# Epsilon of z moved into the bias of the Square, and GpSimd's scaling of t written as one product

## The chip, the cores and the metric

The kernel runs on one core of one Trainium2 chip. The metric is the device time of one execution in microseconds; of the kernel before three runs are known, 151.21, 151.26 and 151.44, with a median of 151.26. The profile is of one further execution, whose instructions span 149.9 us from the first to the last.

Five engines work side by side, each with its own queue of instructions that it takes strictly in order: TensorE (PE in the profile), VectorE (DVE), ScalarE (ACT), GpSimd (POOL) and SyncE (SP, which only issues DMAs here). Between engines there are only semaphores: an instruction adds to one when it is done, and another engine waits until it has reached a count.

## The reference

The input x has 32 sequences of 256 tokens with 128 channels. Two blocks follow each other, both of the form x + layernorm(block(layernorm(x))):

```python
# block 1
A_t = sigmoid(A_param)[:, None] ** t[None, :]
K   = C_vec * A_t * B_vec                       # a causal filter of 256 taps for each channel
out = conv(x_t, K)[..., :L] + D_vec * x_t
out = gelu(out) @ W_proj.T + b_proj
y   = layer_norm(x + out, gamma, beta)          # (z - mean) * rsqrt(var + 1e-5) * gamma + beta
# block 2
xr = mu_r * x + (1 - mu_r) * x_prev             # x_prev: the token before
xk = mu_k * x + (1 - mu_k) * x_prev
out = sigmoid(xr @ W_r.T) * (square(relu(xk @ W_k.T)) @ W_v.T)
```

With the four plain layer norms around the blocks and the one inside block 1 there are five normalisations, and each needs a variance, an epsilon and the power of -0.5 for every token.

## The kernel before

The 8192 tokens are cut into 16 units of 512 (two sequences, four tiles of 128 tokens on the partitions). Everything is fp32 and x stays in SBUF. For one unit u the work is this chain, with the names of the code:

- DVE takes the statistics of x; POOL makes x_r = (var + eps) ** -0.5 and x_bias (`x_scale_of`, for two units at a time); ACT normalises (`normalise`) into xn.
- POOL multiplies xn by powers of A (`xn_times_pow`, 128x512), PE forms prefix sums of it (`prefix_sum`) and transposes xn (`transpose_xn`); DVE turns both into the convolution (`convolve`); ACT applies gelu; PE projects and adds (`project`), which gives z, already with mean zero over the channels, in PSUM (ps_z0 to ps_z2 in turn).
- ACT squares z with a scale of 128 ** -0.5 and adds up along the channels (`square_z`, L397), which gives the variance z_var. POOL adds epsilon (`z_variance`, L248, writing z_ve) and takes the power of -0.5 (`z_root`, L253, writing z_r). DVE uses z_r (`scale_z`), takes the statistics of y, POOL makes yf_r of them, DVE adds y to x (`residual`, giving t) and takes t's statistics.
- POOL makes t_r (`t_variance`, `t_root`). Then t is scaled by t_r into t_scaled: for units 1, 3, 5, 7, 9, 10, 11 and 13 by POOL (`scale_t_pool`, L324), for the others by ACT (`scale_t`, L405). PE transposes it (`transpose_t`, L854), ACT copies it out (`copy_tT`), and PE forms keys, gates and values (L863, L874, L884).
- DVE gates the values, takes statistics of f; POOL makes the last root and out_bias; ACT scales f, POOL subtracts it from x (`add_f`) and SP stores. Units 11, 12, 13 and 15 take a way over DVE at the end.

The order on each engine is written out by hand as one list of calls per engine (L331 to L356 for POOL, L480 on for ACT, L745 on for DVE, L889 on for PE), so that the units run as a staggered pipeline. An engine that meets an unfulfilled wait holds up everything behind it in its list. Buffers come in rings of D = 4 units.

Of the kernel before, what the change touches and what calls it, by code (L numbers as in the profile page):

```python
# [14 lines left out]
def sandwich(nc, x, A_param, B_vec, C_vec, D_vec, W_proj, b_proj, gamma, beta, W_r, W_k, W_v, mu_r, mu_k, out):  # L15
    fp32 = mybir.dt.float32
    ALU = mybir.AluOpType
# [3 lines left out]
    D = 4  # L21
# [9 lines left out]
    with ctx:  # L31
        def sb(name, *shape):
            return ctx.enter_context(nc.sbuf_tensor(name, [P, *shape], fp32))
# [12 lines left out]
        centre = sb("centre", P)  # L46
        prefix_ones = sb("prefix_ones", SEQ)
        neg_half = sb("neg_half", 2 * TILES)
        eps_tile = sb("eps_tile", 2 * TILES)
        zero_col = sb("zero_col", 1)  # L50
        act_warm = sb("act_warm", 2)
        a_col, b_col, c_col, d_col, proj_col, bias_col = (sb(n, 1) for n in (
# [23 lines left out]
        tsT = ring("tsT", 2, SEQ + 1)  # L76
        k_act, tanh, f, f_normal = ring("k_act", UW), ring("tanh", UW), ring("f", UW), ring("f_normal", UW)
        junk = ring("junk", UW)
        z_var, z_ve, z_r = (sb(n, UNITS * TILES) for n in ("z_var", "z_ve", "z_r"))
        t_raw = sb("t_raw", UNITS * TILES, 3)  # L80
        yf_raw = sb("yf_raw", UNITS, 2, TILES, 3)
        yf_r, yf_mean_r = sb("yf_r", UNITS, 2, TILES), sb("yf_mean_r", UNITS, 2, TILES)
# [23 lines left out]
            "xn_ready", "xn_pow_ready", "xT_ready", "xT_copied"))  # L106
        prefix_ready, scaled_ready, conv_ready, gelu_ready = (sem(n) for n in (
            "prefix_ready", "scaled_ready", "conv_ready", "gelu_ready"))
        z_ready, z_squares, z_ve_done, z_scale, z_gamma, y_ready = (sem(n) for n in (
            "z_ready", "z_squares", "z_ve_done", "z_scale", "z_gamma", "y_ready"))  # L110
        y_stats, y_ve_done, y_scale, t_ready = (sem(n) for n in ("y_stats", "y_ve_done", "y_scale", "t_ready"))
        t_stats, t_ve_done, t_scale, ts_ready, ts_pool_ready, tT_ready, tT_copied = (sem(n) for n in (
            "t_stats", "t_ve_done", "t_scale", "ts_ready", "ts_pool_ready", "tT_ready", "tT_copied"))
# [84 lines left out]
        def _(pool):  # L198
# [1 line left out]
            g_.memset(ident[:], 0.0).then_inc(s_filled, 1)  # L200
            g_.memset(prefix_ones[:], 1.0).then_inc(s_filled, 1)
            g_.memset(neg_half[:], -0.5)
            g_.memset(eps_tile[:], EPS)
            for r in range(D):
                g_.memset(tsT[r][:, :, 0:1], 0.0)
            pool.wait_ge(s_filled, 2)
# [26 lines left out]
            def xn_times_pow(u):  # L233
                if u == 0:
                    pool.wait_ge(s_pow, 1)
                pool.wait_ge(xn_ready, u + 1)
                after(pool, prefix_ready, u - D + 1)
                g_.tensor_tensor(xn_pow[u % D][:].rearrange("p (q l) -> p q l", l=SEQ),  # L238
                                 xn[u % D][:].rearrange("p (q l) -> p q l", l=SEQ),
                                 pow_token[:, None, :].to_broadcast([P, 2, SEQ]), ALU.mult).then_inc(xn_pow_ready, 1)  # L240
# [2 lines left out]

                return neg_half[:, 0:n * TILES].rearrange("p (n j) -> p n j", j=TILES)

            def z_variance(u, n):
                pool.wait_ge(z_squares, u + n)
                g_.tensor_tensor(cols(z_ve, u, n), cols(z_var, u, n), eps_tile[:, 0:n * TILES],  # L248
                                 ALU.add).then_inc(z_ve_done, n)

            def z_root(u, n):
                pool.wait_ge(z_ve_done, u + n)
                g_.tensor_tensor(cols(z_r, u, n), cols(z_ve, u, n), neg_half[:, 0:n * TILES],  # L253
                                 ALU.pow).then_inc(z_scale, n)

            def y_variance(u, n):
# [63 lines left out]
            def scale_t_pool(u):  # L320
                pool.wait_ge(t_scale, u + 1)
                after(pool, tT_ready, u - D + 1)
                for j in range(TILES):
                    last = g_.tensor_scalar(tile(t_scaled[u % D], j), xa(u, j), col(t_r, u, j), 1.0, ALU.mult, ALU.mult)  # L324
                last.then_inc(ts_pool_ready, 1)

            def add_f(u):
                pool.wait_ge(f_scaled, u + 1 if u < FUSED[0] else u)
# [2 lines left out]
            x_scale_tiles(0, 0, 2)  # L331
            x_scale_tiles(1, 2, 4)
            x_scale_of(1, 1, 1); xn_times_pow(0); x_scale_of(2, 2, 2); xn_times_pow(1); x_scale_of(3, 4, 2)
            xn_times_pow(2); xn_times_pow(3); z_variance(0, 1); z_root(0, 1); x_scale_of(4, 6, 2); z_variance(1, 1)
            z_root(1, 1); y_variance(0, 1); y_root(0, 1); xn_times_pow(4); x_scale_of(5, 8, 2); y_variance(1, 1)
            t_variance(0, 1); y_root(1, 1); xn_times_pow(5); z_variance(2, 2); t_root(0, 1); z_root(2, 2)
            xn_times_pow(6); t_variance(1, 1); t_root(1, 1); xn_times_pow(7); y_variance(2, 2); y_root(2, 2)
            scale_t_pool(1); xn_times_pow(8); x_scale_of(6, 10, 2); t_variance(2, 2); z_variance(4, 2); t_root(2, 2)
            z_root(4, 2); f_variance(0, 1); f_root(0, 1); scale_t_pool(3); yf_means(0, 1); xn_times_pow(9)
            y_variance(4, 2); out_biases(0, 1); y_root(4, 2); xn_times_pow(10); add_f(0); x_scale_of(7, 12, 2)  # L340
            t_variance(4, 2); z_variance(6, 2); t_root(4, 2); z_root(6, 2); f_variance(1, 1); xn_times_pow(11)
            scale_t_pool(5); f_root(1, 1); yf_means(1, 1); y_variance(6, 2); out_biases(1, 1); y_root(6, 2)
# [16 lines left out]
        def _(act):  # L359
# [568 lines left out]
```

## Time and profile before

| what | value |
|---|---|
| three runs, us | 151.21, 151.26, 151.44 (median 151.26) |
| span of the profiled execution, us | 149.9 |
| PE busy, us | 135.8 (91%) |
| DVE busy, us | 131.5 (88%) |
| ACT busy, us | 129.7 (87%) |
| POOL busy, us | 132.5 (88%) |
| mean granted TensorE clock | 0.984 |

The median of the runs lies 1.36 us above the span of the profiled execution. All four compute engines are busy for nearly nine tenths of the span, so the shares alone do not say which of them sets the end. The chain that ended last and the idle time of an engine before a single instruction, with what ended it, say more. In a row of the timeline stand the start in us, the length in us (of several instructions together where "xN" is above 1), engine, line, operation, output<-inputs, and in brackets the idle time before and what released the engine. The lengths of neighbouring rows can overlap by up to about 0.1 us.

### The profile page before, as it was taken

The numbers are of one execution on the slowest core, as the hardware profiler recorded it, in microseconds if no ns is written. First come the engines' busy times: TensorE is split into PE (matmuls) and PEld (weight loads), VectorE is DVE, ScalarE is ACT, GpSimd is POOL, SyncE is SP. The second block draws the span as 40 slices with busy tenths as digits, with TensorE's granted clock in tenths as the row PEclk, the third lists the DMA queues.
The fourth block names the chain that finished last, engine by engine and source line by source line (L and its number), as shares of the span: only waits on it lengthen the run. The fifth ranks groups of instructions, "written<-read, shape, count | busy, mean of one in ns | idle before, by whom it ended". The sixth has DMA issues, their size and how long they took to land.

```text
span 149.9 us, 3292 instructions
## 1 busy us (share of the span) xinstructions
PE 135.8 (91%) x950; PEld 116.2 (78%) x950; DVE 131.5 (88%) x372; ACT 129.7 (87%) x388; POOL 132.5 (88%) x211
## 2 busy tenths in 40 slices
PE   6777888979999999999999999999999999999900
PEld 6666877867797889797989797988887887777900
DVE  0969899989999998999998999998999899339981
ACT  4869999799879999979779999959998988999940
POOL 4589999999899999999999999888999999999282
PEclk9999999999999999999999999999999999999985
DMA  3999930000000002000200001300200100406524
GB/s 78 239 289 240 294 94 0 0 2 4 0 0 0 0 4 72 0 2 0 74 0 0 0 4 47 98 0 0 77 0 0 56 14 0 142 5 194 157 73 140
DMA packets 18705, 8.99 MB, mean 60 GB/s; under 512 B 1536, under 2 KB 18688, under 8 KB 18688
## 3 DMA queue, kind: packets, MB, share of 16 engines
q1 hardware_dynamic: 17840, 8.52, 20.3%
q10 hardware_dynamic: 848, 0.26, 0.8%
q8 instruction: 8, 0.13, 0.4%
q14 instruction: 9, 0.07, 0.1%
HBM read 4.59 MB, written 4.19 MB: 59 GB/s over the span
## 4 chain that ended last, share of the span: by engine, by line
PE 70%; POOL 17%; DMA 3%; issue 2%; DVE 2%; SPq 2%; POOLq 1%
PE ps_k L863 9%; PE ps_k L864 9%; PE ps_r L875 9%; PE ps_r L874 9%; PE ps_tv L884 9%; PE ps_z L841 7%; POOL xn_pow L238 5%; PE ps_tv L854 4%; POOL x_r L229 4%; PE ps_prefix L821 4%; DMA x_all<-in_x 3%; PE ps_z L842 3%; PE ps_xT L813 3%; POOL z_r L253 2%; PE ps_prefix L827 2%
## 5 line engine op out<-in xcount | busy, mean ns | idle before, releaser
L377 ACT ACTIVATE xn<-x_all,x_bias,x_r 128x128 f32<-128x128 f32 x64 | 26.4, 494 | 0.6 <-POOL x_bias L220 0.6
L875 PE MATMUL ps_r<-mixed_T,tsT 128*128 128x128 f32 x128 | 24.7, 275 | 0.0
L874 PE MATMUL ps_r<-mixed_T,tsT 128*128 128x128 f32 x128 | 24.7, 275 | 0.0
L841 PE MATMUL ps_z<-pv_T,gelu 128*128 128x128 f32 x128 | 22.1, 275 | 0.0
L434 ACT ACTIVATE f_normal<-f,out_bias,yf_r 128x128 f32<-128x128 f32 x48 | 19.7, 492 | 1.6 <-POOL out_bias L292 1.6
L238 POOL TENSOR_TENSOR xn_pow<-xn,pow_token 128x512 f32<-128x512 f32 x16 | 20.3, 1272 | 0.0
L874 PEld LDWEIGHTS ps_r<-mixed_T,tsT 128*128 128x128 f32 x128 | 19.5, 192 | 0.5 <-issue 0.5
L841 PEld LDWEIGHTS ps_z<-pv_T,gelu 128*128 128x128 f32 x128 | 19.4, 191 | 0.5 <-issue 0.5
L397 ACT ACTIVATE junk<-ps_z 128x128 f32<-128x128 f32 x64 | 16.7, 277 | 3.2 <-PE ps_z L842 3.2
L875 PEld LDWEIGHTS ps_r<-mixed_T,tsT 128*128 128x128 f32 x128 | 19.4, 192 | 0.0
L580 DVE SCALAR_TENSOR_TENSOR ps_z<-ps_z,z_r,beta_row 128x128 f32<-128x128 f32 x64 | 17.5, 353 | 0.5 <-POOL z_r L253 0.5
L592 DVE SCALAR_TENSOR_TENSOR x_all<-ps_z,yf_r,x_all 128x128 f32<-128x128 f32 x64 | 17.4, 344 | 0.2 <-POOL yf_r L263 0.2
L842 PE MATMUL ps_z<-ident,xnT 128*128 128x128 f32 x64 | 17.4, 273 | 0.0
L884 PEld LDWEIGHTS ps_tv<-pv_T,k_act 128*128 128x128 f32 x124 | 15.4, 192 | 1.9 <-issue 1.9
L821 PE MATMUL ps_prefix<-prefix_ones,xn_pow 128*128 128x256 f32 x48 | 14.8, 389 | 2.0 <-POOL xn_pow L238 1.9
L863 PE MATMUL ps_k<-tsT,mixed_T 128*128 128x512 f32 x32 | 16.5, 599 | 0.0
L884 PE MATMUL ps_tv<-pv_T,k_act 128*128 128x128 f32 x124 | 16.4, 275 | 0.0
L864 PE MATMUL ps_k<-tsT,mixed_T 128*128 128x512 f32 x32 | 16.3, 592 | 0.0
L329 POOL TENSOR_TENSOR x_all<-x_all,f_normal 128x512 f32<-128x512 f32 x12 | 15.2, 1277 | 0.3 <-ACT f_normal L434 0.3
L263 POOL TENSOR_TENSOR yf_r<-y_ve,neg_half 128x8 f32<-128x8 f32 (+1 forms) x10 | 13.9, 1390 | 0.6 <-issue 0.2
L253 POOL TENSOR_TENSOR z_r<-z_ve,neg_half 128x8 f32<-128x8 f32 (+1 forms) x10 | 13.8, 1385 | 0.6
L272 POOL TENSOR_TENSOR t_r<-t_ve,neg_half 128x8 f32<-128x8 f32 (+1 forms) x10 | 13.9, 1387 | 0.2
(114 smaller groups left out, 365.7 us busy)
## 6 DMA issues: line engine op xcount, KB each, us to landing
out_x<-x_all SPq DMA_DIRECT2D x15, 256.0 KB, 2.3
x_all<-in_x SPq DMA_DIRECT2D x7, 512.0 KB, 6.3
x_all<-in_x SPq DMA_DIRECT2D x2, 128.0 KB, 2.9
x_all<-in_x SPq DMA_DIRECT2D x1, 256.0 KB, 3.3
out_x<-x_all SPq DMA_DIRECT2D x1, 128.0 KB, 1.8
out_x<-x_all ACTq DMA_DIRECT2D x1, 128.0 KB, 1.9
w_pv<-in_W_proj ACTq DMA_DIRECT2D x1, 64.0 KB, 3.5
w_pv<-in_W_v ACTq DMA_DIRECT2D x1, 64.0 KB, 4.3
```

The source lines that it names most:

```text
L238: g_.tensor_tensor(xn_pow[u % D][:].rearrange("p (q l) -> p q l", l=SEQ), xn[u % D][:].rearrange("p (q l) -> p q l", l=SEQ), pow_token[:, ...
L377: last = a_.activation(tile(xn[u % D], j), xa(u, j), ACT.Identity, bias=col(x_bias, u, j), scale=col(x_r, u, j))
L434: last = a_.activation(tile(f_normal[u % D], j), tile(f[u % D], j), ACT.Identity, bias=out_bias[:, u, j:j + 1], scale=yf_r[:, u, 1, j:j + 1])
L580: last = v_.scalar_tensor_tensor(tile(ps_z[u % 3], j), tile(ps_z[u % 3], j), col(z_r, u, j), beta_row[:], ALU.mult, ALU.add)
L821: t_.matmul(ps_prefix[:, q * SEQ:(q + 1) * SEQ], tile(xn_pow[u % D], 2 * q), prefix_ones[:], start=True, stop=False)
L841: t_.matmul(tile(ps_z[u % 3], j), tile(gelu[u % D], j), pv_T[:, 0, :], start=True, stop=False)
L842: last = t_.matmul(tile(ps_z[u % 3], j), tile(xnT[u % D], j), ident[:], is_transpose=True, start=False, stop=True)
L863: t_.matmul(k_out, mixed_T[:, 2, :], tsT[u % D][:, :, 1:SEQ + 1], start=True, stop=False)
L864: t_.matmul(k_out, mixed_T[:, 3, :], tsT[u % D][:, :, 0:SEQ], start=False, stop=True).then_inc(k_ready, 1)
L874: t_.matmul(tile(ps_r, j), tsT[u % D][:, q, l + 1:l + 1 + P], mixed_T[:, 0, :], start=True, stop=False)
L875: last = t_.matmul(tile(ps_r, j), tsT[u % D][:, q, l:l + P], mixed_T[:, 1, :], start=False, stop=True)
L884: last = t_.matmul(tile(bank, j), tile(k_act[u % D], j), pv_T[:, 1, :], start=True, stop=True)
```

## The change

Two things are rewritten; what is computed stays the same up to rounding.

First, epsilon of z. The sum over the channels of (z / sqrt(128) + b) ** 2 is the variance plus 2 b / sqrt(128) times the sum of z plus 128 b ** 2. The sum of z is zero, and with b = sqrt(eps / 128) the last term is eps. So the Square gets this number as its bias, its accumulated output is the variance with epsilon in it, and the ten calls of `z_variance` go with their tile z_ve, their constant tile eps_tile and their semaphore. `z_root` now waits for the Squares itself. The Squares no longer wait for z_ve.

Second, `scale_t_pool`: four scalings of 128x128 by a column of t_r become one product of 128x512 with the four columns of t_r broadcast along the channels.

```diff
@@ POOL
-            g_.memset(eps_tile[:], EPS)
...
-            def z_variance(u, n):
+            def z_root(u, n):
                 pool.wait_ge(z_squares, u + n)
-                g_.tensor_tensor(cols(z_ve, u, n), cols(z_var, u, n), eps_tile[:, 0:n * TILES],
-                                 ALU.add).then_inc(z_ve_done, n)
-
-            def z_root(u, n):
-                pool.wait_ge(z_ve_done, u + n)
-                g_.tensor_tensor(cols(z_r, u, n), cols(z_ve, u, n), neg_half[:, 0:n * TILES],
+                g_.tensor_tensor(cols(z_r, u, n), cols(z_var, u, n), neg_half[:, 0:n * TILES],
                                  ALU.pow).then_inc(z_scale, n)
...
             def scale_t_pool(u):
                 pool.wait_ge(t_scale, u + 1)
                 after(pool, tT_ready, u - D + 1)
-                for j in range(TILES):
-                    last = g_.tensor_scalar(tile(t_scaled[u % D], j), xa(u, j), col(t_r, u, j), 1.0, ALU.mult, ALU.mult)
-                last.then_inc(ts_pool_ready, 1)
+                g_.tensor_tensor(t_scaled[u % D][:].rearrange("p (j c) -> p j c", c=P),
+                                 xa(u, 0, TILES).rearrange("p (j c) -> p j c", c=P),
+                                 cols(t_r, u)[:, :, None].to_broadcast([P, TILES, P]), ALU.mult).then_inc(ts_pool_ready, 1)
...
-            t_variance(0, 1); y_root(1, 1); xn_times_pow(5); z_variance(2, 2); t_root(0, 1); z_root(2, 2)
+            t_variance(0, 1); y_root(1, 1); xn_times_pow(5); t_root(0, 1); z_root(2, 2)
...
@@ ACT
             def square_z(u):
                 act.wait_ge(z_ready, u + 1)
-                after(act, z_ve_done, u - D + 1)
...
-                    last = a_.activation(tile(junk[u % D], j), tile(ps_z[u % 3], j), ACT.Square, scale=float(P) ** -0.5,
-                                         accum_out=col(z_var, u, j))
+                    last = a_.activation(tile(junk[u % D], j), tile(ps_z[u % 3], j), ACT.Square, bias=(EPS / P) ** 0.5,
+                                         scale=float(P) ** -0.5, accum_out=col(z_var, u, j))
```

The calls of `z_variance` are struck from POOL's list and nothing else in it changes place. How POOL's instructions then stand is seen at two places, and ACT's at one. The first place is on POOL, from the powers of units 2 and 3 to the root of y of unit 0 (z_r with four columns is one unit's root). Before:

```order
L238 TENSOR_TENSOR xn_pow<-xn,pow_token 128x512 x2
L248 TENSOR_TENSOR z_ve<-z_var,eps_tile 128x4
L253 TENSOR_TENSOR z_r<-z_ve,neg_half 128x4
L226 TENSOR_SCALAR x_v<-x_raw 128x8
L227 TENSOR_SCALAR x_neg<-x_raw 128x8
L229 TENSOR_TENSOR x_r<-x_v,neg_half 128x8
L231 TENSOR_TENSOR x_bias<-x_neg,x_r 128x8
L248 TENSOR_TENSOR z_ve<-z_var,eps_tile 128x4
L253 TENSOR_TENSOR z_r<-z_ve,neg_half 128x4
L258 TENSOR_SCALAR y_ve<-yf_raw 128x4
```

The same place on POOL after the change:

```order
L236 TENSOR_TENSOR xn_pow<-xn,pow_token 128x512 x2
L246 TENSOR_TENSOR z_r<-z_var,neg_half 128x4
L224 TENSOR_SCALAR x_v<-x_raw 128x8
L225 TENSOR_SCALAR x_neg<-x_raw 128x8
L227 TENSOR_TENSOR x_r<-x_v,neg_half 128x8
L229 TENSOR_TENSOR x_bias<-x_neg,x_r 128x8
L246 TENSOR_TENSOR z_r<-z_var,neg_half 128x4
L251 TENSOR_SCALAR y_ve<-yf_raw 128x4
```

Two additions of epsilon are gone, and the roots of z read the Squares' sums directly. The second place is on POOL, from the powers of unit 5 to the scaling of t of unit 1 (z_r with eight columns is of units 2 and 3). Before:

```order
L238 TENSOR_TENSOR xn_pow<-xn,pow_token 128x512
L248 TENSOR_TENSOR z_ve<-z_var,eps_tile 128x8
L272 TENSOR_TENSOR t_r<-t_ve,neg_half 128x4
L253 TENSOR_TENSOR z_r<-z_ve,neg_half 128x8
L238 TENSOR_TENSOR xn_pow<-xn,pow_token 128x512
L267 TENSOR_SCALAR t_ve<-t_raw 128x4
L272 TENSOR_TENSOR t_r<-t_ve,neg_half 128x4
L238 TENSOR_TENSOR xn_pow<-xn,pow_token 128x512
L258 TENSOR_SCALAR y_ve<-yf_raw 128x8
L263 TENSOR_TENSOR yf_r<-y_ve,neg_half 128x2x4
L324 TENSOR_SCALAR t_scaled<-x_all,t_r 128x128 x4
```

The same place on POOL after the change:

```order
L236 TENSOR_TENSOR xn_pow<-xn,pow_token 128x512
L265 TENSOR_TENSOR t_r<-t_ve,neg_half 128x4
L246 TENSOR_TENSOR z_r<-z_var,neg_half 128x8
L236 TENSOR_TENSOR xn_pow<-xn,pow_token 128x512
L260 TENSOR_SCALAR t_ve<-t_raw 128x4
L265 TENSOR_TENSOR t_r<-t_ve,neg_half 128x4
L236 TENSOR_TENSOR xn_pow<-xn,pow_token 128x512
L251 TENSOR_SCALAR y_ve<-yf_raw 128x8
L256 TENSOR_TENSOR yf_r<-y_ve,neg_half 128x2x4
L316 TENSOR_TENSOR t_scaled<-x_all,t_r 128x512
```

The addition of epsilon and its wait for the Squares of unit 3 no longer stand ahead of t_r of unit 0, and t_scaled is one instruction with two tensors as its inputs. The third place is on ACT, around the Squares of unit 0 after the change; a bias or a scale that is a tile stands among an instruction's inputs:

```order
L370 ACTIVATE xn<-x_all,x_bias,x_r 128x128 x4
L384 ACTIVATE gelu<-conv 128x512
L379 ACTIVATE xnT<-ps_xT,bias_col 128x512
L370 ACTIVATE xn<-x_all,x_bias,x_r 128x128 x4
L389 ACTIVATE junk,z_var<-ps_z 128x128 x4
```

Nothing moved there: the Squares read ps_z alone, as before, and their new bias is a number in the instruction, not a tile.

## Rows read from the trace of the kernel before

**Rows 1.** Page, chain of work that ended last: shares of the span by engine.

```profile
PE 70%; POOL 17%; DMA 3%; issue 2%; DVE 2%; SPq 2%; POOLq 1%
```

**Rows 2.** Busy time by stretch: stretch and length, then busy us (instructions) per engine.

```profile
10.30:35.45 25.15, 21.22 (x156) 18.81 (x154) 23.70 (x60) 22.99 (x79) 23.87 (x35) 1.00 0.40 105
35.45:140.05 104.60, 104.60 (x733) 88.21 (x734) 95.97 (x269) 95.84 (x288) 98.00 (x146) 1.00 0.10 30
140.05:149.90 9.85, 2.74 (x25) 2.55 (x23) 6.07 (x18) 4.13 (x10) 4.55 (x9) 0.76 0.40 121
```

**Rows 3.** Timeline of PE, 31 to 43 us: start, length, engine, line, operation.

```profile
31.47 0.70 PE L821 MATMUL ps_prefix<-prefix_ones,xn_pow 128*128 128x256 f32 x2 [0.99 <-POOL xn_pow L238]
...
34.21 0.60 PE L854 MATMUL ps_tv<-ident,t_scaled 128*128 128x128 f32 x4
34.71 0.63 PE L813 MATMUL ps_xT<-ident,xn 128*128 128x128 f32 x4
35.45 0.70 PE L821 MATMUL ps_prefix<-prefix_ones,xn_pow 128*128 128x256 f32 x2
...
42.11 0.60 PE L854 MATMUL ps_tv<-ident,t_scaled 128*128 128x128 f32 x4
```

**Rows 4.** Timeline of POOL, 18 to 42 us.

```profile
18.85 0.20 POOL L248 TENSOR_TENSOR z_ve<-z_var,eps_tile 128x4 f32<-128x4 f32 x1
19.13 1.01 POOL L253 TENSOR_TENSOR z_r<-z_ve,neg_half 128x4 f32<-128x4 f32 x1
...
22.55 0.20 POOL L248 TENSOR_TENSOR z_ve<-z_var,eps_tile 128x4 f32<-128x4 f32 x1
22.82 1.01 POOL L253 TENSOR_TENSOR z_r<-z_ve,neg_half 128x4 f32<-128x4 f32 x1
...
31.38 0.20 POOL L248 TENSOR_TENSOR z_ve<-z_var,eps_tile 128x8 f32<-128x8 f32 x1
31.54 1.00 POOL L272 TENSOR_TENSOR t_r<-t_ve,neg_half 128x4 f32<-128x4 f32 x1
...
34.12 1.28 POOL L238 TENSOR_TENSOR xn_pow<-xn,pow_token 128x512 f32<-128x512 f32 x1
...
40.21 1.43 POOL L324 TENSOR_SCALAR t_scaled<-x_all,t_r 128x128 f32<-128x128 f32 x4
```

**Rows 5.** Timeline of ACT, 32 and 77 us: two waits.

```profile
32.58 1.28 ACT L405 ACTIVATE t_scaled<-x_all,t_r 128x128 f32<-128x128 f32 x4 [0.29 <-POOL t_r L272]
...
77.49 0.69 ACT L386 ACTIVATE xnT<-ps_xT,bias_col 128x512 f32<-128x512 f32 x1 [0.84 <-PE ps_xT L813]
```

**Rows 6.** Timeline of DVE at 33 us, the first half of convolution 5.

```profile
33.09 0.69 DVE L550 TENSOR_TENSOR conv_scaled<-ps_prefix,pow_down 128x512 f32<-128x512 f32 x1 [0.47 <-PE ps_prefix L823]
```

**Rows 7.** Waits of POOL: who waited for whom, us in total, times, longest.

```profile
POOL x_r L218 <- DVE x_v L526: 2.2, 1, 2.2
```

**Rows 8.** Timeline of DVE, 133 to 141 us.

```profile
133.75 0.70 DVE L619 SCALAR_TENSOR_TENSOR ps_z<-tanh,ps_tv 128x512 f32<-128x512 f32 x1 [3.35 <-ACT tanh L427]
...
137.22 0.69 DVE L634 TENSOR_TENSOR ps_z<-ps_z,yf_raw 128x512 f32<-128x512 f32 x1
137.92 0.69 DVE L610 TENSOR_TENSOR x_all<-x_all,ps_xT 128x512 f32<-128x512 f32 x1
138.75 1.13 DVE L654 SCALAR_TENSOR_TENSOR x_all<-ps_z,yf_r,x_all 128x128 f32<-128x128 f32 x4
...
140.58 0.68 DVE L605 SCALAR_TENSOR_TENSOR f<-tanh,ps_tv 128x512 f32<-128x512 f32 x1
```

**Rows 9.** Timeline of POOL at 137 us, the root of f of units 12 and 13.

```profile
136.98 1.63 POOL L282 TENSOR_TENSOR yf_r<-f_ve,neg_half 128x8 f32<-128x8 f32 x1
```

**Rows 10.** Groups of ACT's instructions: line, operation, xcount, busy us, mean ns.

```profile
L397 ACT ACTIVATE junk<-ps_z 128x128 f32<-128x128 f32 x64 | 16.7, 277 | 3.2 <-PE ps_z L842 3.2
...
L386 ACT ACTIVATE xnT<-ps_xT,bias_col 128x512 f32<-128x512 f32 x16 | 11.0, 685 | 3.5 <-PE ps_xT L813 3.5
...
L412 ACT ACTIVATE tsT<-ps_tv 128x512 f32<-128x512 f32 x16 | 9.4, 590 | 1.8 <-PE ps_tv L854 1.8
```

More of the change, by code:

```diff
@@ L48, in sandwich @@
         neg_half = sb("neg_half", 2 * TILES)
-        eps_tile = sb("eps_tile", 2 * TILES)
         zero_col = sb("zero_col", 1)
@@ L78, in sandwich @@
         junk = ring("junk", UW)
-        z_var, z_ve, z_r = (sb(n, UNITS * TILES) for n in ("z_var", "z_ve", "z_r"))
+        z_var, z_r = (sb(n, UNITS * TILES) for n in ("z_var", "z_r"))
         t_raw = sb("t_raw", UNITS * TILES, 3)
@@ L108, in sandwich @@
             "prefix_ready", "scaled_ready", "conv_ready", "gelu_ready"))
-        z_ready, z_squares, z_ve_done, z_scale, z_gamma, y_ready = (sem(n) for n in (
-            "z_ready", "z_squares", "z_ve_done", "z_scale", "z_gamma", "y_ready"))
+        z_ready, z_squares, z_scale, z_gamma, y_ready = (sem(n) for n in (
+            "z_ready", "z_squares", "z_scale", "z_gamma", "y_ready"))
         y_stats, y_ve_done, y_scale, t_ready = (sem(n) for n in ("y_stats", "y_ve_done", "y_scale", "t_ready"))
@@ L333, in _ @@
             x_scale_of(1, 1, 1); xn_times_pow(0); x_scale_of(2, 2, 2); xn_times_pow(1); x_scale_of(3, 4, 2)
-            xn_times_pow(2); xn_times_pow(3); z_variance(0, 1); z_root(0, 1); x_scale_of(4, 6, 2); z_variance(1, 1)
+            xn_times_pow(2); xn_times_pow(3); z_root(0, 1); x_scale_of(4, 6, 2)
             z_root(1, 1); y_variance(0, 1); y_root(0, 1); xn_times_pow(4); x_scale_of(5, 8, 2); y_variance(1, 1)
-            t_variance(0, 1); y_root(1, 1); xn_times_pow(5); z_variance(2, 2); t_root(0, 1); z_root(2, 2)
+            t_variance(0, 1); y_root(1, 1); xn_times_pow(5); t_root(0, 1); z_root(2, 2)
@@ L337, in _ @@
             xn_times_pow(6); t_variance(1, 1); t_root(1, 1); xn_times_pow(7); y_variance(2, 2); y_root(2, 2)
-            scale_t_pool(1); xn_times_pow(8); x_scale_of(6, 10, 2); t_variance(2, 2); z_variance(4, 2); t_root(2, 2)
+            scale_t_pool(1); xn_times_pow(8); x_scale_of(6, 10, 2); t_variance(2, 2); t_root(2, 2)
             z_root(4, 2); f_variance(0, 1); f_root(0, 1); scale_t_pool(3); yf_means(0, 1); xn_times_pow(9)
             y_variance(4, 2); out_biases(0, 1); y_root(4, 2); xn_times_pow(10); add_f(0); x_scale_of(7, 12, 2)
-            t_variance(4, 2); z_variance(6, 2); t_root(4, 2); z_root(6, 2); f_variance(1, 1); xn_times_pow(11)
+            t_variance(4, 2); t_root(4, 2); z_root(6, 2); f_variance(1, 1); xn_times_pow(11)
@@ L342, in _ @@
             scale_t_pool(5); f_root(1, 1); yf_means(1, 1); y_variance(6, 2); out_biases(1, 1); y_root(6, 2)
-            xn_times_pow(12); add_f(1); x_scale_of(8, 14, 2); z_variance(8, 2); z_root(8, 2); f_variance(2, 2)
+            xn_times_pow(12); add_f(1); x_scale_of(8, 14, 2); z_root(8, 2); f_variance(2, 2)
             t_variance(6, 2); xn_times_pow(13); t_root(6, 2); scale_t_pool(7); y_variance(8, 2); y_root(8, 2)
             xn_times_pow(14); f_root(2, 2); xn_times_pow(15); yf_means(2, 2); t_variance(8, 2); out_biases(2, 2)
-            z_variance(10, 2); z_root(10, 2); add_f(2); t_root(8, 2); add_f(3); y_variance(10, 2); f_variance(4, 2)
+            z_root(10, 2); add_f(2); t_root(8, 2); add_f(3); y_variance(10, 2); f_variance(4, 2)
@@ L347, in _ @@
             y_root(10, 2); scale_t_pool(9); f_root(4, 2); yf_means(4, 2); out_biases(4, 2); t_variance(10, 2)
-            z_variance(12, 2); z_root(12, 2); add_f(4); t_root(10, 2); scale_t_pool(10); y_variance(12, 2)
-            f_variance(6, 2); y_root(12, 2); f_root(6, 2); z_variance(14, 1); yf_means(6, 2); z_root(14, 1)
-            out_biases(6, 2); scale_t_pool(11); t_variance(12, 2); z_variance(15, 1); t_root(12, 2); add_f(5)
+            z_root(12, 2); add_f(4); t_root(10, 2); scale_t_pool(10); y_variance(12, 2)
@@ L351, in _ @@
+            f_variance(6, 2); y_root(12, 2); f_root(6, 2); yf_means(6, 2); z_root(14, 1)
+            out_biases(6, 2); scale_t_pool(11); t_variance(12, 2); t_root(12, 2); add_f(5)
             z_root(15, 1); y_variance(14, 1); f_variance(8, 2); y_root(14, 1); f_root(8, 2); yf_means(8, 2)
```

## Prediction

> **What bounds the kernel now.** I read the chain that ended last first: TensorE holds 70% of it and GpSimd 17% [rows 1]. The reader is to ask where these two parts lie, since only GpSimd is to lose work. The busy time by stretch answers it [rows 2]. From 35.45 us to 140.05 us PE is busy for 104.60 of 104.60 us: whatever the others save there, PE has no idle time to give up, and this stretch can only move as a block. Before it, from 10.30 to 35.45, PE is busy for 21.22 of 25.15 us and POOL for 23.87. PE's own timeline names what it waits for there: 0.99 us for POOL's xn_pow ahead of the prefix sum of unit 5 at 31.47, and at 35.45, where the dense stretch begins, the prefix sum of unit 6 starts 0.05 us after xn_pow of unit 6 ends at 34.12 + 1.28 = 35.40 [rows 3, 4]. So POOL's queue sets when PE's block begins, PE sets when it ends, and after 140.05 a chain over DVE, POOL and ACT closes the kernel.
>
> **The change part by part.** Removed are ten additions of epsilon, three of them ahead of 35.45. What one is worth there is the step from its start to that of the next instruction in POOL's queue, since nothing else was awaited:
> - unit 0: 18.85 to 19.13, 0.28 us; unit 1: 22.55 to 22.82, 0.27 us. The root that follows needs the sum, so the handing over within POOL goes too.
> - units 2 and 3: 31.38 to 31.54, 0.16 us; here t_r of unit 0 stood between, and no handing over was seen [rows 4].
>
> Together 0.71 us, of which 0.55 fall ahead of xn_pow of unit 5 and all 0.71 ahead of xn_pow of unit 6, which then ends at 34.69.
>
> Does PE take it? The prefix sum of unit 5 goes from 31.47 to 30.92, since PE had been idle for 0.99 us. The project of unit 4 and the transposes of t of unit 0 follow on PE, the latter at 34.21 - 0.55 = 33.66. They need t_scaled from ACT. ACT began it at 32.58 after 0.29 us of waiting for t_r [rows 5]; t_r now comes 0.55 + 0.16 us earlier, so ACT begins at 32.29 and ends 1.28 us later at 33.57, just in time. The transposes of xn of unit 6 started at 34.71. They also need convolution 5 by DVE. Its first half waited 0.47 us for the prefix sum of unit 5 [rows 6], so DVE can move by that 0.47 and no more; the transposes start at 34.24 and, with the 0.44 us that the four of t take before them (34.21 to 34.65), leave PE free at 34.68. xn_pow of unit 6 is handed over at 34.74. So POOL is still last, by 0.06 us, and PE's block begins 0.71 us earlier. A handful of hundredths decide here, so the lower end of this term is the 0.47 of DVE.
>
> The seven other additions of epsilon, 0.20 us each, lie beside PE's full block and give nothing by themselves. The same holds for the removed memset of eps_tile at the start: POOL waits 2.2 us for DVE right after its setup [rows 7]. The twelve waits that ACT loses were for sums long done; I take nothing for them, and a gain would be hidden behind PE as well.
>
> Added is the bias of the Square. No row shows a Square with one. From below, ACT's copies show what an operand can cost: 685 ns for 512 elements with bias_col as the bias, 590 ns without it, so 95 ns for each; the Square now takes 277 ns [rows 10]. The bound is 0 to 95 ns. The new bias is a number that the instruction carries, where the old one carried a zero, and its inputs are the same single tile, so I take 0. The Trainium skill has the same distinction (ScalarE: Activation LUTs, What ACT_TABLE_LOAD costs): immediate scale and bias are the base price and each column operand adds about 93 ns; the 95 ns of this trace agrees, and by that rule this bias adds nothing.
>
> Moved is the scaling of t on POOL, eight times: four scalings took 1.43 us in all, a product of two 128x512 tensors (xn_pow, one of them broadcast over the sequences) takes 1.28 [rows 4]. What no row of POOL shows is an input that stands still along the innermost dimension. On DVE such a product costs nothing extra: 0.69 us for centring by a broadcast column at 137.22, 0.69 us for the plain subtraction behind it [rows 8]. I take 1.28; the range for it is 1.28 to 2.56, the latter if both halves of the traffic doubled. The first product has the least room: t_scaled of unit 1 began at 40.21, and I let it come only DVE's 0.47 earlier, at 39.74. PE wants it at 42.11 - 0.71 = 41.40 [rows 3]. So it may take 1.6 us before PE feels it, and eight times 0.15 us saved beside PE's block are worth nothing.
>
> The Trainium skill has a rule that could speak against this (GPSIMD Engine Reference, Performance pitfalls for Q7 kernels): an inner step of more than 8 bytes makes a read about half as dear again. A step of zero is not named there. No run here shows it on POOL; as an estimate by that page's factor the product would take 1.28 x 1.5 = 1.92 us, 0.3 us beyond what unit 1 has room for.
>
> At the end, what moves with PE is ACT's tanh of unit 13, for which DVE waits 3.35 us at 133.75; the DVE chain after it sets the end. In it add_fused (138.75) begins 0.14 us after DVE's instruction before is over (137.92 + 0.69 = 138.61), and POOL's root of f ends at 138.61 too [rows 8, 9]. POOL is further ahead by then, so I count these 0.14 us as gained: gate(14) at 140.58 follows on DVE, and the statistics, roots and store follow on it.
>
> **Sum.** 0.71 + 0.14 = 0.85 us off the profiled span of 149.9, which becomes about 149.05. The median of the runs lies 1.36 us above that span, before the first and after the last instruction, where nothing changes: 151.26 - 0.85 = 150.4.
>
> **Rivals.**
> - DVE cannot follow. Only 0.47 us of the advance survives because the convolutions feed PE through the block's first units and DVE is busy there nearly as much as PE (95.97 of 104.60 us) [rows 2]. 151.26 - 0.47 = 150.8. Against it: DVE has 8.6 us of idle time in the block.
> - The gain is given back inside the block: ACT (95.84 of 104.60 us) does not move, and PE waits for it until it is where it was. 151.26, no change. Against it: ACT itself waits for PE within the block, 0.84 us at 77.49 [rows 5], so it follows PE rather than leads.
> - The product with a broadcast column is dear on POOL. At 1.92 us (the factor of the skill's rule) unit 1's transposes lose 0.3 us, 8 x 0.49 - 7 x 0.2 = 2.5 us more POOL work vanish in its 6.6 us of idle time, and 0.55 us of 0.85 remain: 150.7. At 2.56 us unit 1 ends at 42.30, 0.9 us too late, and the 0.71 are more than lost; 8 x 1.13 - 1.4 = 7.6 us of additional work exceed the 6.6 us of idle time by 1.0: 151.26 + 0.2 to + 1.0, some 152, and up to 157 if the idle time cannot be used because it sits in waits. It turns slower above 39.74 + 2.3 us. For it speaks only that no row of POOL shows the pattern; against it the DVE row.
> - The Square's bias is fetched like a column after all: 64 x 95 ns = 6.1 us on ACT, which has 8.8 us idle in the block. Between nothing lost and 4 us lost, some 153. Against it: the instruction has no second tile.
>
> **How the numbers follow.** Forecast (150.1 to 150.6): 0.58. DVE follows by half, or a product of about 1.9 us (150.6 to 150.9): 0.18. Given back (151.0 to 151.5): 0.14. Dear product: 0.07. Dear bias: 0.03. What a measurement of this kernel can tell from no change is about 0.2%, 0.3 us. So faster 0.76, same 0.14, slower 0.10. The range leaves out the two slower cases and what of the forecast's spread lies beneath it: 150.1 to 151.2; the likeliest case's own is 150.1 to 150.6.
>
> **What would show it.** Right: POOL's z_r of unit 0 begins near 18.85, xn_pow of unit 6 near 33.4, PE's prefix sum of unit 6 near 34.74, PE's waits in the block stay absent, and its dense stretch is 104.6 us long; Squares of 277 ns; t_scaled in one instruction of about 1.28 us. Wrong: Squares nearer 370 ns, t_scaled above 1.6 us with PE idle before the transposes at L854, or a PE block that begins earlier and ends where it did. If the block begins 0.7 us earlier and the end does not, the step that failed is that ACT and DVE follow PE.

## The result, and the profile after

The changed kernel takes 150.28 us (median of 4 runs, 150.21 to 150.56) against 151.24 us before on the same chip (151.13 to 151.44): a ratio of 0.9932, 95% interval 0.9915 to 0.9949, so 0.96 us less by the medians (0.77 to 1.29 by the interval). The forecast was 150.4. The profiled execution took 150.25 us, its span 148.5 us (149.9 before; why the spans differ by more than the times is told further down).

The busy time by stretch, cut where PE's dense stretch begins and as many microseconds behind (columns as in [rows 2]):

```profile
10.30:34.20 23.90, 20.94 (x154) 18.66 (x153) 23.06 (x59) 22.42 (x78) 22.93 (x31) 1.00 0.35 104
34.20:138.80 104.60, 104.60 (x734) 88.20 (x734) 95.38 (x270) 96.14 (x289) 93.62 (x115) 1.00 0.10 30
138.80:148.50 9.70, 2.75 (x25) 2.56 (x23) 6.05 (x17) 4.14 (x10) 4.55 (x9) 0.81 0.41 121
```

PE's dense stretch is as long as before, 104.60 us without idle time; it begins at 34.20 and not at 35.45, 1.25 us earlier. POOL does 4.4 us less in it, 93.62 for 98.00, and the stretch is no shorter for it. The time came from ahead of the stretch. POOL's timeline there (start, length, operation):

```profile
10.28 1.65 POOL L227 TENSOR_TENSOR x_r<-x_v,neg_half 128x8 f32<-128x8 f32 x1
...
18.31 1.01 POOL L246 TENSOR_TENSOR z_r<-z_var,neg_half 128x4 f32<-128x4 f32 x1
...
21.73 1.01 POOL L246 TENSOR_TENSOR z_r<-z_var,neg_half 128x4 f32<-128x4 f32 x1
...
31.27 1.64 POOL L246 TENSOR_TENSOR z_r<-z_var,neg_half 128x8 f32<-128x8 f32 x1
32.87 1.28 POOL L236 TENSOR_TENSOR xn_pow<-xn,pow_token 128x512 f32<-128x512 f32 x1
...
38.99 1.04 POOL L316 TENSOR_TENSOR t_scaled<-x_all,t_r 128x512 f32<-128x512 f32 x1
```

and the same x_r in the kernel before:

```profile
10.82 1.65 POOL L229 TENSOR_TENSOR x_r<-x_v,neg_half 128x8 f32<-128x8 f32 x1
```

From x_r of units 2 and 3 to xn_pow of unit 6, POOL needed 34.12 - 10.82 = 23.30 us before [rows 4] and needs 32.87 - 10.28 = 22.59 now: 0.71 less. Another 0.54 us lie ahead of that x_r: POOL begins the whole queue earlier. PE, DVE and ACT at the places of [rows 3, 5, 6]:

```profile
30.39 0.70 PE L813 MATMUL ps_prefix<-prefix_ones,xn_pow 128*128 128x256 f32 x2 [0.46 <-POOL xn_pow L236]
...
33.63 0.63 PE L805 MATMUL ps_xT<-ident,xn 128*128 128x128 f32 x4
34.20 0.70 PE L813 MATMUL ps_prefix<-prefix_ones,xn_pow 128*128 128x256 f32 x2
```

```profile
31.59 1.30 ACT L397 ACTIVATE t_scaled<-x_all,t_r 128x128 f32<-128x128 f32 x4
```

```profile
32.01 0.69 DVE L542 TENSOR_TENSOR conv_scaled<-ps_prefix,pow_down 128x512 f32<-128x512 f32 x1
```

PE's wait for xn_pow of unit 5 fell from 0.99 to 0.46 us, and the waits of ACT (0.29) and DVE (0.47) are gone. The prefix sum of unit 6 again starts 0.05 us after its xn_pow ends (32.87 + 1.28 = 34.15), so POOL still sets the start of the stretch.

What came earlier ahead of x_r is seen on POOL's x_v, which needs DVE's statistics, and on DVE, which waits for the loads of x. POOL before (the same x_v is at 9.84 after, without a wait, right behind xn_pow, which ends at 9.76):

```profile
10.37 0.20 POOL L226 TENSOR_SCALAR x_v<-x_raw 128x8 f32<-128x8 f32 x1 [0.49 <-DVE x_raw L514]
```

DVE's statistics of units 2 to 5, before:

```profile
8.85 1.43 DVE L514 BATCH_NORM_STATS2 x_raw<-x_all 128x6 f32<-128x256 f32 x4 [0.85 <-DMA x_all<-in_x]
10.62 1.43 DVE L514 BATCH_NORM_STATS2 x_raw<-x_all 128x6 f32<-128x256 f32 x4 [0.34 <-DMA x_all<-in_x]
```

and after, with a shorter wait for the first load and none for the second:

```profile
8.26 2.95 DVE L506 BATCH_NORM_STATS2 x_raw<-x_all 128x6 f32<-128x256 f32 x8 [0.38 <-DMA x_all<-in_x]
```

At the end of the kernel (DVE, then POOL):

```profile
136.69 0.69 DVE L602 TENSOR_TENSOR x_all<-x_all,ps_xT 128x512 f32<-128x512 f32 x1 [0.27 <-ACT ps_xT L438]
137.47 1.13 DVE L646 SCALAR_TENSOR_TENSOR x_all<-ps_z,yf_r,x_all 128x128 f32<-128x128 f32 x4
```

```profile
134.17 0.28 POOL L270 TENSOR_SCALAR f_ve<-yf_raw 128x8 f32<-128x8 f32 x1 [0.95 <-DVE yf_raw L506]
134.42 1.31 POOL L322 TENSOR_TENSOR x_all<-x_all,f_normal 128x512 f32<-128x512 f32 x1
135.69 1.63 POOL L275 TENSOR_TENSOR yf_r<-f_ve,neg_half 128x8 f32<-128x8 f32 x1
```

The sum f_ve ahead of that root needs DVE's statistics of f; first before (DVE, then POOL), then DVE's after:

```profile
134.49 0.76 DVE L514 BATCH_NORM_STATS2 yf_raw<-ps_z 128x6 f32<-128x256 f32 x2
135.57 0.21 POOL L277 TENSOR_SCALAR f_ve<-yf_raw 128x8 f32<-128x8 f32 x1
```

```profile
133.25 0.76 DVE L506 BATCH_NORM_STATS2 yf_raw<-ps_z 128x6 f32<-128x256 f32 x2
```

add_fused comes at 137.47 for 138.75 [rows 8], 1.28 us earlier, and the root of f at 135.69 for 136.98 [rows 9], 1.29: hardly more than the 1.25 of PE. POOL's last add_f, behind which the last store goes, begins at 144.62 (145.90 before), 111.75 us after xn_pow of unit 6, before 111.78.

### The profile page after: what moved, and what is told of

It reads as the page before. It is cut to its first block, busy times and chain, and to the rows that moved or that the text cites. A ratio compares the mean times of both kernels' runs of the same rounds, so it can differ in the third digit from the quotient of the medians.

```text
span 148.5 us, 3239 instructions
## 1 busy us (share of the span) xinstructions
PE 135.5 (91%) x950; PEld 116.0 (78%) x950; DVE 130.8 (88%) x372; ACT 129.6 (87%) x388; POOL 127.5 (86%) x176
## 4 chain that ended last, share of the span: by engine, by line
PE 73%; POOL 17%; DVE 4%; DMA 2%; issue 1%; POOLq 1%; ACT 0%
PE ps_k L855 9%; PE ps_k L856 9%; PE ps_r L867 9%; PE ps_r L866 9%; PE ps_tv L876 9%; PE ps_z L833 7%; POOL x_r L227 5%; POOL xn_pow L236 5%; PE ps_tv L846 5%; PE ps_prefix L813 4%; PE ps_z L834 4%; PE ps_xT L805 3%; PE ps_prefix L819 2%; PE ps_prefix L815 2%; DMA a_col<-in_A_param 2%
## 5 line engine op out<-in xcount | busy, mean ns | idle before, releaser
L246 POOL TENSOR_TENSOR z_r<-z_var,neg_half 128x8 f32<-128x8 f32 (+1 forms) x10 | 13.8, 1385 | 1.3 <-ACT junk L389 1.1
```

## The experiments

Three distances measure every kernel below: POOL from x_r of units 2 and 3 to xn_pow of unit 6 (**the queue**), from there to POOL's last add_f (**the rest**), and the time at which that x_r begins, which the loads of x set. Ratios are to the kernel before, in runs on the same chip. They are not the quotients of the medians, from which they differ by up to 0.0012; gains in us that are given with a ratio are worked out from the ratio. Theory: the 0.71 us of the first three additions and nothing else of the change. Rivals: the product or the seven later additions have a part in it; or part of the gain is the place of the tiles, since the two dropped tiles shift others and the loads land at another time.

**z_only**: epsilon in the Square, the four scalings kept. **t_only**: the reverse.

```diff
 z_only, against the changed kernel
-                g_.tensor_tensor(t_scaled[u % D][:].rearrange("p (j c) -> p j c", c=P), ...
+                for j in range(TILES):
+                    last = g_.tensor_scalar(tile(t_scaled[u % D], j), xa(u, j), col(t_r, u, j), 1.0, ALU.mult, ALU.mult)
+                last.then_inc(ts_pool_ready, 1)
```

> Epsilon of z in the Square's bias as in the changed kernel, t scaled by four operations as before. Theory 1 (only the three additions ahead of PE's dense block count): the whole gain, 0.75 us off before, about the time of the changed kernel, 150.3 to 150.5. Rival 2 (every microsecond that POOL loses counts in proportion): the additions are 2.0 to 2.3 us of the 5.0 us of busy time that POOL lost, so some 0.4 us off, 150.8. Rival 3 (the loads of x land earlier because tiles were removed): the xn_pow of unit 6 begins more than 0.71 us before 34.12 in this kernel too.

> Epsilon added by POOL as before, t scaled by one product. Theory 1: no change, 151.1 to 151.4, although POOL is 3.1 us less busy; PE's dense block begins near 35.4 as before. Rival 2: 60% of the gain, some 0.55 us off, 150.7.

z_only: 150.42 us, ratio 0.9937 (0.9915 to 0.9958); queue 22.59, rest 111.81. t_only: 151.37, ratio 0.9993 (0.9979 to 1.0007); queue 23.31, rest 111.77. The product gives nothing that can be measured, the epsilon nearly all.

**z_first**: epsilon in the Square for units 0 to 3 only (the first three additions). **z_later**: for units 4 to 15 only (the other seven). Both keep eps_tile and z_ve, and so every tile's place, and both leave out the Squares' wait for z_ve, as the change does.

```diff
 z_first, against the kernel before
             def z_variance(u, n):
+                if u < 4:
+                    return
...
+                                         bias=(EPS / P) ** 0.5 if u < 4 else 0.0,
```

> The kernel before with epsilon in the Square's bias for units 0 to 3 alone (three additions gone); from unit 4 on POOL adds it as before. Theory 1: the whole gain, 0.7 us off, 150.4 to 150.6. Rival 2: three of ten additions, 0.1 us off, 151.1.

> The kernel before with epsilon in the Square's bias for units 4 to 15 alone (seven additions gone). Theory 1: no change, 151.1 to 151.4. Rival 2: 0.3 us off, 150.95.

z_first: 150.64, ratio 0.995 (0.9933 to 0.9967); queue 22.58, rest 111.81. z_later: 151.40, ratio 0.9999 (0.9983 to 1.0014); queue 23.31, rest 111.81. Three additions give 0.0050 x 151.56 = 0.76 us, seven give none.

**eps_twice**: the kernel before, each of the first three additions made twice, the second into an unused tile.

```diff
+        z_v2 = sb("z_v2", UNITS * TILES)
...
                                  ALU.add).then_inc(z_ve_done, n)
+                if u < 4:
+                    pool.wait_ge(z_ve_done, u + n)
+                    g_.tensor_tensor(cols(z_v2, u, n), cols(z_ve, u, n), eps_tile[:, 0:n * TILES], ALU.add)
```

> The kernel before with a second addition behind each of the first three (units 0, 1 and 2 with 3), its output unused. Theory 1: POOL's queue sets the start of PE's block, so each costs its step, 0.16 + 0.16 + 0.28 = 0.6 us slower than before, 151.85 where before has 151.25. Rival 2: three more of some 130 us of POOL work, 0.1 us slower.

152.07, ratio 1.0031 (1.0018 to 1.0044): 0.47 us more. The queue grew by 0.56 to 23.86, the rest stayed (111.77). PE shows where it lands, at the prefix sum of unit 6:

```profile
35.71 0.48 PE L825 MATMUL ps_prefix<-prefix_ones,xn_pow 128*128 128x256 f32 x1 [0.38 <-POOL xn_pow L239]
```

So time in POOL's queue ahead of the stretch counts in both directions: 0.76 us of gain (0.50 to 1.02) for 0.72 less in the queue of z_first, 0.47 of loss (0.27 to 0.67) for 0.56 more here.

**after_again** is the changed kernel once more; **layout** is it with the two dropped tiles still allocated, unused.

```diff
         neg_half = sb("neg_half", 2 * TILES)
+        eps_tile = sb("eps_tile", 2 * TILES)
...
-        z_var, z_r = (sb(n, UNITS * TILES) for n in ("z_var", "z_r"))
+        z_var, z_ve, z_r = (sb(n, UNITS * TILES) for n in ("z_var", "z_ve", "z_r"))
```

> The changed kernel unaltered, as the yardstick for the others of this set: 0.7 to 1.0 us below before. Theory 1 in the trace: from x_r of units 2 and 3 to xn_pow of unit 6 on POOL 22.59 us (23.30 in the kernel before), from xn_pow of unit 6 to the last addition on POOL 111.8 us as before; what differs beyond that lies in when the loads of x arrive.

> The changed kernel with the two dead tiles (eps_tile, z_ve) still allocated, so that all tiles behind them stand at the addresses of the kernel before; nothing uses them. Theory 1: the same as the changed kernel within 0.1 us. Rival 3 (0.2 us and more of the gain comes from where the tiles lie, by loads that land earlier): 0.2 to 0.5 us slower than the changed kernel, 150.6 to 150.8 where that has 150.3.

after_again: 150.24, ratio 0.9918 (0.9902 to 0.9934). layout: 150.68, ratio 0.9946 (0.993 to 0.9962), though it executes the same instructions: queue 22.58 and rest 111.72 in both. Only what comes ahead of x_r differs (it begins at 10.37, and at 10.26 in after_again). DVE in layout:

```profile
8.41 1.42 DVE L507 BATCH_NORM_STATS2 x_raw<-x_all 128x6 f32<-128x256 f32 x4 [0.55 <-DMA x_all<-in_x]
10.22 1.43 DVE L507 BATCH_NORM_STATS2 x_raw<-x_all 128x6 f32<-128x256 f32 x4 [0.39 <-DMA x_all<-in_x]
```

and in after_again:

```profile
7.94 2.93 DVE L506 BATCH_NORM_STATS2 x_raw<-x_all 128x6 f32<-128x256 f32 x8
```

The theory had layout within 0.1 us of the changed kernel, the rival of the place 0.2 to 0.5 us slower, and it came out 0.44 slower. The intervals just overlap, so three more kernels test the place alone. eps_tile takes 32 bytes of each partition ahead of x_all: without it x_all begins at byte 31,744, with it at 31,776. **before_moved** is the kernel before with both tiles allocated last, **after_pad32** and **after_pad64** the changed kernel with an unused tile of 32 or 64 bytes in eps_tile's place.

```diff
 before_moved
-        eps_tile = sb("eps_tile", 2 * TILES)
...
         fused_y = sb("fused_y", TILES)
+        eps_tile = sb("eps_tile", 2 * TILES)
+        z_ve = sb("z_ve", UNITS * TILES)
 after_pad64
         neg_half = sb("neg_half", 2 * TILES)
+        pad = sb("pad", 4 * TILES)
```

> The kernel before, with eps_tile and z_ve allocated behind all other tiles, so that x_all begins at byte 31,744 of each partition, as after the change, and not at 31,776; every instruction stays. Theory (the place of x_all, 32 bytes past a multiple of 64 in the kernel before and on one after, makes the loads of x land sooner and gives the part of the gain that the 0.71 us of POOL does not): 0.2 to 0.45 us faster than before, and DVE's second wait for loads of x (0.33 to 0.39 us) gone. Rival (the landing of loads varies from run to run, and the gain is POOL's alone): within 0.1 us of before.

> The changed kernel with an unused tile of 32 bytes for each partition ahead of x_all, which puts x_all back at 31,776; every instruction stays. Theory (place of x_all): 0.2 to 0.45 us slower than the changed kernel, near 150.6, with two waits of DVE for loads of x. Rival (variation): within 0.1 us of the changed kernel.

> The changed kernel with an unused tile of 64 bytes ahead of x_all, which puts it at 31,808, on a multiple of 64 again; every instruction stays. If the remainder by 64 decides: as the changed kernel, near 150.25, one wait of DVE for loads of x or none. If it is the larger multiple of 512 that 31,744 lies on, or any shift: as the one with 32 bytes, near 150.6.

before_moved: 151.30, ratio 0.9984 (0.9972 to 0.9996), 0.24 us less (0.06 to 0.42) with every instruction kept; queue 23.35, rest 111.88. DVE in it:

```profile
8.24 2.92 DVE L515 BATCH_NORM_STATS2 x_raw<-x_all 128x6 f32<-128x256 f32 x8 [0.37 <-DMA x_all<-in_x]
```

after_pad32: 150.79, ratio 0.9948 (0.993 to 0.9966); queue 22.62, rest 111.76. after_pad64: 150.84, ratio 0.9952 (0.9935 to 0.9969); queue 22.59, rest 111.72. DVE in after_pad64:

```profile
8.28 1.43 DVE L507 BATCH_NORM_STATS2 x_raw<-x_all 128x6 f32<-128x256 f32 x4 [0.36 <-DMA x_all<-in_x]
10.13 1.43 DVE L507 BATCH_NORM_STATS2 x_raw<-x_all 128x6 f32<-128x256 f32 x4 [0.43 <-DMA x_all<-in_x]
```

So 32 bytes past a multiple of 64 is not what is slow, as I had thought; 64 bytes do the same. All kernels together:

| x_all begins at | kernels | DVE's second wait for loads of x | POOL's x_r begins at, mean |
|---|---|---|---|
| 31,744 | after, after_again, z_only, reorder2, before_moved, forms_bias | none, 6 of 6 | 10.26 to 10.78, 10.38 |
| 31,776 | before, t_only, z_first, z_later, eps_twice, layout, after_pad32 | 0.33 to 0.39 us, 7 of 7 | 10.37 to 10.99, 10.65 |
| 31,808 | after_pad64 | 0.43 us | 10.30 |

The times at which the loads land, which the traces keep as well, show what is behind the second wait: the load of units 4 and 5 (512 KB) lands 1.47 to 1.53 us behind that of units 2 and 3 in all six kernels at 31,744, and 1.73 to 1.86 us behind it in all eight at the two later places (in the rows of layout, DVE begins at 8.41 and 10.22, each time 0.02 us after the landing). So loads follow each other more slowly there, and DVE, which needs 1.43 us for a pair of units, has to wait again. The second wait costs no time by itself: after_pad64 has it, and its x_r begins at 10.30, no later than POOL alone would begin it (its profiled execution was the fastest of its seven, 150.53 us). What costs is the first wait, where it lets POOL's x_v wait. POOL alone would begin x_r near 10.28, and the eight kernels of the two later places begin it at 10.60 on average, those at 31,744 at 10.38: 0.22 us, near the 0.24 of before_moved. These are single executions of each kernel, and z_only shows that x_r can be late at 31,744 too (10.78). The slower loads and the times are measured; that the time is lost by way of the first wait is argued.

And with the shorter queue: z_first, layout, after_pad32 and after_pad64, all at the two later places, lie at 0.9946 to 0.9952; z_only, after, after_again and reorder2, at 31,744, at 0.9915 to 0.9937. The two groups do not overlap, though single intervals do.

**reorder2**: an attempt at a better version. The changed kernel with xn_pow of units 5 and 6 moved up in POOL's queue, ahead of the x scale of units 8 and 9, and PE's prefix sum of unit 6 ahead of its transposes.

```diff
-            z_root(1, 1); y_variance(0, 1); y_root(0, 1); xn_times_pow(4); x_scale_of(5, 8, 2); y_variance(1, 1)
-            t_variance(0, 1); y_root(1, 1); xn_times_pow(5); t_root(0, 1); z_root(2, 2)
-            xn_times_pow(6); t_variance(1, 1); t_root(1, 1); ...
+            z_root(1, 1); y_variance(0, 1); y_root(0, 1); xn_times_pow(4); xn_times_pow(5); y_variance(1, 1)
+            t_variance(0, 1); y_root(1, 1); t_root(0, 1); xn_times_pow(6); z_root(2, 2)
+            x_scale_of(5, 8, 2); t_variance(1, 1); t_root(1, 1); ...
...
-            project(4); transpose_t(0); transpose_xn(6); prefix_sum(6); ...
+            project(4); transpose_t(0); prefix_sum(6); transpose_xn(6); ...
```

> The changed kernel with POOL's scaling factors of x for units 8 and 9 (2.2 us of POOL) moved behind z_r of units 2 and 3 and the powers of units 5 and 6 moved up, and on PE the prefix sum of unit 6 ahead of the transposes of xn of unit 6. Theory 1 with the rows of the changed kernel: POOL is then no longer last; PE's prefix sum of unit 5 starts near 29.8 in its clock, the transposes of t of unit 0 wait for ACT until 32.95 instead of 33.14, the prefix sum of unit 6 follows at 33.4, the keys of unit 0 at 35.14 instead of 35.62: 0.4 to 0.5 us faster than the changed kernel, about 149.85. Rival (DVE's convolution 5 holds PE all the same): the same time as the changed kernel.

150.17, ratio 0.9915 (0.9897 to 0.9934): not to be told from the changed kernel, where the theory said 149.85. PE's keys (ps_k) begin at 35.17 for 35.58 in after_again, 0.41 us earlier; the last add_f at 144.43 for 144.56, 0.13 earlier. Of the 0.28 us lost between, 0.20 go at one place. PE in reorder2:

```profile
39.98 0.60 PE L805 MATMUL ps_xT<-ident,xn 128*128 128x128 f32 x4
40.63 0.55 PE L846 MATMUL ps_tv<-ident,t_scaled 128*128 128x128 f32 x3
```

and POOL:

```profile
39.54 1.04 POOL L316 TENSOR_TENSOR t_scaled<-x_all,t_r 128x512 f32<-128x512 f32 x1
```

The transposes of xn end near 40.42 (four took 0.44 us, 40.39 to 40.83, in after_again); PE then idles until t_scaled of unit 1 is there at 39.54 + 1.04 = 40.58. The x scale that was moved back stands ahead of that product in POOL's queue: in after_again it was there at 38.95 + 1.04 = 39.99. PE begins these transposes at 40.63 for 40.83 in after_again, 0.20 earlier; the remaining 0.07 us go behind them, and where was not looked for.

**forms_bias**: prices of operations, in the changed kernel. Four kinds of product or scaling stand in the place of the scaling of t, so that it leaves out the right scaling for units 1, 3, 5, 7, 11 and 13, and the Square takes its bias from a column of a tile.

```diff
...
+                if u in (1, 3):
...
+                    last = g_.tensor_tensor(out, x_in, gamma_row[:, None, :].to_broadcast([P, TILES, P]), ALU.mult)
+                elif u in (5, 7):
...
+                    last = g_.tensor_tensor(out, x_in, mixers[:], ALU.mult)
+                elif u in (9, 10):
+                    last = g_.tensor_tensor(out, x_in, cols(t_r, u)[:, :, None].to_broadcast([P, TILES, P]), ALU.mult)
+                else:
+                    last = g_.tensor_scalar(out, x_in, col(t_r, u, 0), 1.0, ALU.mult, ALU.mult)
...
-                    last = a_.activation(..., ACT.Square, bias=(EPS / P) ** 0.5,
+                    last = a_.activation(..., ACT.Square, bias=eps_col[:],
```

> Prices of operations in the changed kernel; the scaling of t is left out for units 1, 3, 5, 7, 11 and 13, where POOL makes a 128x512 product of another kind: units 1 and 3 with a row broadcast over the tiles, 5 and 7 with a full tensor, 9 and 10 with the column broadcast along each tile as in the change, 11 and 13 one scaling with a single column for all 512 elements. And the Square takes its bias from a column tile, not from a number. If an input that stands still makes the product cheaper: units 9 and 10 near 1.04 us, the other products near 1.27. If xn_pow's 1.27 us come from its pow_token tile or its place and not from the kind: all products near 1.04. One scaling of 512 elements: 0.9 to 1.1 us by the four of 128 at 0.37 each (1.42 together). Square: 277 ns to about 370 if a column costs what it costs ACT's copies (685 against 590 ns), 280 if not; with 64 of them ACT would be busy for up to 6 us more, and the time up to 3 us longer.

Groups of POOL's instructions (line, operation, shapes, count, busy us, mean ns), then of ACT's:

```profile
L325 POOL TENSOR_TENSOR t_scaled<-x_all,mixers 128x512 f32<-128x512 f32 x2 | 2.6, 1278 | 0.1
L322 POOL TENSOR_TENSOR t_scaled<-x_all,gamma_row 128x512 f32<-128x512 f32 x2 | 2.5, 1273 | 0.0
L327 POOL TENSOR_TENSOR t_scaled<-x_all,t_r 128x512 f32<-128x512 f32 x2 | 2.1, 1042 | 0.1
L329 POOL TENSOR_SCALAR t_scaled<-x_all,t_r 128x512 f32<-128x512 f32 x2 | 1.4, 700 | 0.2
```

```profile
L401 ACT ACTIVATE junk<-ps_z,eps_col 128x128 f32<-128x128 f32 x64 | 22.7, 374 | 2.4 <-PE ps_z L846 2.4
```

A product with a column broadcast along each tile takes 1.04 us, one with a moving second input 1.27 to 1.28, whether that is a row broadcast over the tiles or a full tensor. A Square with a column as bias takes 374 ns, with a number 280 in the changed kernel: 94 ns. The one run took 151.64 us, 1.4 more than the changed kernel. It holds both edits, so how much of this is the bias stays open, but part of it is: the queue, in which no scaling of t stands, is 22.91 us and so 0.32 longer, 0.24 of it a wait of POOL's root of unit 1 for the Squares. ACT was busy for 134.6 us, 5.0 more, and POOL for 128.1, 0.6 more.

## Why the prediction was right

**The 0.71 us ahead of the stretch** were right to the hundredth: 23.30 - 22.59. z_first has this part alone and gains 0.76 us (0.50 to 1.02), z_later shows the other seven additions at nothing, and eps_twice pays for POOL's time there as z_first gains by it. That POOL stays last, with DVE and ACT just able to follow, held too: neither waits any more.

**That the stretch moves as a block** held: 104.60 us in both, so neither "DVE cannot follow" nor "given back inside the block" came true. POOL's saved 4.4 us within it turned into waits. POOL's, after (waited for: us in total, times, longest):

```profile
POOL f_ve L270 <- DVE yf_raw L506: 4.4, 5, 2.6
...
POOL y_ve L251 <- DVE yf_raw L506: 1.7, 3, 0.9
POOL x_all L322 <- ACT f_normal L426: 1.6, 3, 0.7
POOL z_r L246 <- ACT junk L389: 1.1, 2, 0.7
```

In the kernel before the first three are 2.8, 0.2 and 0.3 us in total, and POOL's wait for the Squares is 0.3. The longest of f_ve, 2.6, lies behind the stretch in both.

**The Square's bias** at nothing was right: 280 ns for 277 [rows 10]. The rival's price was right as well for what it assumed: a column costs 94 ns in forms_bias, against the 95 read from ACT's copies. The Trainium skill (ScalarE: Activation LUTs, What ACT_TABLE_LOAD costs) gives about 93 ns for a column operand and none for an immediate one; these runs agree on both.

**The product** was worth nothing, as forecast (t_only), but its price was not in the range: 1.04 us, below the lower bound of 1.28. The bound came from xn_pow, whose second input moves, and I had excluded a gain without a reason. The rival of a dear product fell: the factor of 1.5 that the Trainium skill gives for an inner step of more than 8 bytes (GPSIMD Engine Reference, Performance pitfalls for Q7 kernels), by which I had estimated 1.92 us, is not what a step of zero costs here: 1.04 us against 1.27 to 1.28 with moving inputs.

**The 0.14 us at the end** is the term that was mis-sized: 0.03 came in this pair (111.78 - 111.75). Over the kernels of the experiments the rest is 111.72 to 111.76 in the five with both parts of the change, in the order of the change, and 111.77 to 111.88 in the seven with one part or none: 0.07 apart on average, half of what I had taken. I had read that add_fused waits for POOL's root of f, which is so in both profiles: the root ends at 135.69 + 1.63 = 137.32, add_fused begins at 137.47. But I took the root to come early once POOL was ahead of its queue. POOL was ahead, and idled 0.95 us at 134.17, since the sum ahead of that root needs DVE's statistics, which follow ACT's tanh and so PE. It began 0.32 us behind the end of those statistics before (135.57 - 135.25) and 0.16 behind it now (134.17 - 134.01), so POOL's lead had about 0.16 us to give there, and add_f (1.31 us) still stands between that sum and the root in the queue. A second reason appears beside it: DVE's step ahead of add_fused now waits 0.27 us for ACT.

**What the sum did not hold** is the place of x_all. The queue and the end together give 0.71 + 0.03 = 0.74 us, 0.78 with the 0.07, and the four kernels with this queue at the two later places gain 0.0048 to 0.0054 of 151.6 us, 0.73 to 0.82. The other 0.2 us of the 0.96 are about what x_all at 31,744 is worth: before_moved gains 0.24 (0.06 to 0.42) by that alone. Thus the 150.28, 0.12 under the forecast: about 0.1 too much at the end, about 0.2 left out at the start. That the number came so near is in part luck, since the two errors point in opposite directions, and the 0.96 itself is not known to a tenth: after_again gained 1.24 us (1.00 to 1.49). In the two profiled executions the start differed by 0.54 us, more than the 0.2: x_r begins anywhere from 10.30 to 10.99 at the later places, and the execution of before was one of the late ones. That z_r of unit 0 began at 18.31 and not near 18.85, and the prefix sum of unit 6 at 34.20 and not 34.74, is this 0.54.

**The 1.36 us between median and span** were misread. They are no fixed part before the first and after the last instruction: wherever the time and the span of one execution are both on record, they lie 1.69 to 2.08 us apart. The 1.36 set the median of the runs against a profiled execution that was late. It stands on both sides of the sum and so drops out of the forecast; that late execution is also why the two spans differ by 1.4 us and the medians by 0.96.

What stays open: why loads follow each other more slowly at 31,776 and 31,808. x_all at 31,744 begins on a multiple of 512 bytes (62 x 512), the length of a row of x; the other two are multiples of 32 and 64 bytes and of no higher power of two. Which power from 128 on decides, or whether another tile that moved along has a part, was not tried.

## What to carry to other kernels

When one engine has no idle time in a long stretch, price an edit by where the others let that stretch begin and by what follows it: three additions ahead of it gave all of POOL's 0.71 us, and seven additions or eight scalings beside it, taken alone, gave nothing that could be measured. At the end, ask of each instruction that waits what its releaser itself waits for, since freeing an engine's queue does not bring an input earlier. And compare a kernel that drops a tile with one that keeps it unused, before the difference is credited to the instructions.

## What the hardware showed that I had not expected

- On POOL a 128x512 product with one input standing still along each tile took 1.04 us, with two moving inputs 1.27 to 1.28; one scaling by a single column for 512 elements took 0.70, four of 128 elements 1.43 [rows 4].
- With the target of the loads 32 or 64 bytes of each partition further on, a load of 512 KB landed 1.73 to 1.86 us behind the one before it in 8 of 8 kernels, against 1.47 to 1.53 us in 6 of 6 at 31,744, and DVE waited for loads a second time, 0.33 to 0.43 us. Allocating the two tiles of the kernel before behind all others gave 0.24 us (0.06 to 0.42).
